# A wait for the landing of the preceding list write, in a fused attention and mixture-of-experts kernel

## The reference

```python
x = layernorm(x + attention(x))        # x: 16 sequences x 256 tokens x 256 features; 16 heads of 16
x = layernorm(x + ffn(x))              # 4096 tokens, 8 experts, 2 experts to a token

# ffn
capacity = ceil(4096 * 2 / 8 * 1.25)   # 1280 slots per expert
gates = softmax(x_flat @ gating_w)
topk_w, topk_idx = top_k(gates, 2)
norm_w = topk_w / (sum(topk_w) + 1e-8)
position = running count of the items of each expert     # the slot of an item
buf[expert, position] = x_flat[token]                    # dropped where position >= capacity
h = relu(buf @ w1 + b1)                                  # 256 -> 1024
out_e = h @ w2 + b2                                      # 1024 -> 256
out[token] += out_e[expert, position] * norm_w           # for both experts of a token
```

## Time and profile before

| | |
|---|---|
| time, median of 3 runs | 821.24 us (820.07 to 822.61) |
| span of the profiled execution | 856.8 us |
| PE, DVE, ACT, POOL busy | 92%, 71%, 52%, 48% of the span |
| mean granted clock of PE | 0.971 of full speed |

### The profile page before, as it was taken

How to read it: one execution, slowest core, us unless ns; L and a number is a source line. 1 busy time by engine, 2 the same in 40 slices (tenths; PEclk the granted TensorE clock), 3 DMA queues, 4 the chain that set the end, 5 groups by cost and what they waited for, 6 DMA issues and landing times.

```text
span 856.8 us, 16628 instructions
## 1 busy us (share of the span) xinstructions
PE 784.5 (92%) x5919; PEld 648.5 (76%) x5919; DVE 605.1 (71%) x1325; ACT 442.1 (52%) x753; POOL 410.2 (48%) x595
## 2 busy tenths in 40 slices
PE   7699989999989985896999999999999999999994
PEld 7577766677667653585889898898898888988993
DVE  5768878888888885683756856756657568665983
ACT  3166757777666664542534534534345345443670
POOL 1011245555555546457146445254364462556675
PEclk9799999999999998799899999999999999999998
DMA  5677765555555572326145245253352451533741
GB/s 158 135 165 161 161 153 113 114 113 114 116 114 110 115 141 73 116 51 180 20 91 109 41 89 115 43 130 50 81 111 40 96 112 31 140 57 57 288 179 46
DMA packets 71534, 92.75 MB, mean 108 GB/s; under 512 B 12972, under 2 KB 55885, under 8 KB 71324
## 3 DMA queue, kind: packets, MB, share of 16 engines
q1 hardware_dynamic: 53308, 67.95, 31.0%
q0 software_dynamic: 16928, 22.15, 14.9%
q10 hardware_dynamic: 1216, 1.57, 0.8%
HBM read 39.18 MB, written 26.89 MB: 77 GB/s over the span
## 4 chain that ended last, share of the span: by engine, by line
PE 69%; DVE 14%; issue 5%; POOL 3%; another core or an unknown queue 3%; DMA 2%; ACT 2%; ACTq 1%; POOLq 0%; DVEq 0%; SPq 0%
PE bank L1718 14%; DVE negm L890 10%; PE wide L1687 8%; PE wide L1685 8%; PE wide L1686 8%; PE bank L985 7%; PE bank L1720 7%; PE wide L1030 5%; PE bank L1664 2%; PE wide L1048 2%; PE bank L1095 2%; PE bank L1064 1%; PE bank L994 1%; POOL slot_list L533 1%
## 5 line engine op out<-in xcount | busy, mean ns | idle before, releaser
L1359 POOL DMA_INDIRECT acc_rows<-o_w,lists x70 | 120.4, 1720 | 181.6 <-ACT o_w L1508 167.9
L890 DVE TENSOR_REDUCE negm<-wide 128x4 f32<-128x1024 f32 x128 | 156.1, 1222 | 50.5 <-PE wide L1030 31.7
L630 ACT ACTIVATE probs<-wide 128x1024 f32<-128x1024 f32 x128 | 131.0, 1024 | 89.1 <-PE wide L1048 68.9
L1475 ACT ACTIVATE h<-wide,b1T 128x512 f32<-128x512 f32 (+1 forms) x200 | 115.0, 600 | 96.8 <-PE wide L1687 69.1
L1720 PE MATMUL bank<-stack,h_lo 128*128 128x256 f32 x560 | 156.9, 280 | 0.0
L1685 PE MATMUL wide<-g_hi,stack 128*128 128x512 f32 (+1 forms) x400 | 140.8, 352 | 5.2 <-DVE g_lo L1536 4.1
L1687 PE MATMUL wide<-g_hi,stack 128*128 128x512 f32 (+1 forms) x400 | 140.1, 350 | 0.1
L1686 PE MATMUL wide<-g_lo,stack 128*128 128x512 f32 (+1 forms) x400 | 140.1, 350 | 0.0
L1508 ACT ACTIVATE o_w<-o_b,lists 128x256 f32<-128x256 f32 x70 | 35.7, 510 | 148.6 <-DVE o_b L1646 135.5
L1718 PE MATMUL bank<-stack,h_hi 128*128 128x512 f32 x304 | 108.7, 401 | 1.3 <-DVE o_b L1646 1.3
L1720 PEld LDWEIGHTS bank<-stack,h_lo 128*128 128x128 f32 x560 | 105.6, 189 | 0.0
(11 more groups left out here) (211 smaller groups left out, 1640.9 us busy)
## 6 DMA issues: line engine op xcount, KB each, us to landing
stack<-qk SPq DMA_DIRECT2D x180, 128.0 KB, 4.2
w_raw<-in_L_ffn_w SPq DMA_DIRECT2D x16, 1024.0 KB
x_sb<-in_L_attn_x SPq DMA_DIRECT2D x16, 256.0 KB, 5.1
x_rows<-x SPq DMA_DIRECT2D x16, 256.0 KB
acc_rows<-x SPq DMA_DIRECT2D x16, 256.0 KB
acc_sb<-acc_rows SPq DMA_DIRECT2D x8, 512.0 KB, 11.1
out<-acc_sb SPq DMA_DIRECT2D x8, 512.0 KB
x_rows<-zrow SPq DMA_DIRECT2D x2, 1152.0 KB, 6.6
```

Of the source, the lines that this page charges most:

```text
L630: nc.scalar.activation(probs[:, i % 4].rearrange("p x c t -> p x (c t)"), shifted_banks(i)[:, :, :], ACT.Exp, scale=SCALE).then_inc(exp_do ...
L890: nc.vector.tensor_reduce(negm[n % 2][:, :, :, u].rearrange("p c x -> p x c"), score_banks(PAIRS * n + u)[:, :, :].rearrange("p x (c t) -> ...
L1359: nc.gpsimd.indirect_dma_start(out=acc_d, out_offset=bass.IndirectOffsetOnAxis(ap=lists[:, e, QC * c + r, 0:1], axis=0), in_=o_w[c][:, r, ...
L1475: ins = nc.scalar.activation(h[u % 2][:, t], banks[BZ[u % 4]][:, t], ACT.Relu, bias=b1T[:, FT * e + f:FT * e + f + 1])
```

## The change

Before each list write of a sequence but its first (c = 0, k = 0), POOL waits until the semaphore of the sequence has the count that it has when all of its earlier writes have landed: 16 for each of the four writes of each earlier sequence on that semaphore, and 16 for each earlier write of this one. Nothing else is changed.

```diff
@@ -530,6 +530,8 @@
                 pool.wait_ge(token_done, m + 1)
                 pool.wait_ge(weight_done, m + 1)
                 for k in range(TOPK):
+                    if c or k:
+                        pool.wait_ge(listed[m % 4], 16 * (QC * TOPK * (m // 4) + TOPK * c + k))
                     nc.gpsimd.indirect_dma_start(
                         out=list_d, out_offset=bass.IndirectOffsetOnAxis(ap=dest[m % 4][:, c, k:k + 1], axis=0),
                         in_=item[m % 4][:, c, k, :], in_offset=None, bounds_check=NE * CAP - 1,
```

## The result

The changed kernel takes 882.79 us (881.62 to 884.7, four runs), the kernel before 821.92 us beside it (820.07 to 822.8): a ratio of 1.0756 [1.0738, 1.0774], 61 us slower. The forecast was slower at 870 us, with a range of 836 to 900.

What follows compares the result with a forecast made beforehand. PE was 92% busy; POOL had about 6.8 us to spare per attention sequence, none in the hand-over. 24 + 28 = 52 us on 856.8 gave 909 us; scaled by 0.9585, 871, stated as 870 us, range 836 to 900.

Steps and rivals of the forecast that it cites:

- both stages pay: Attention and hand-over to the experts: the main forecast, waits cost 24 + 28 us; chance 62%, own range 843 to 888 us.
- pitch: POOL's list writes: start of one write to the next, 4.1 us with the wait in place of 1.27 us.
- The prediction's estimate by the Trainium skill's figure: List writes: fixed 2.0 us with 0.55 us to restart, pitch 2.55 us; sum some 7 us in place of 52.
- Attention stage: One sequence every 20 us: waits exceed POOL's 6.8 us idle, 2.7 us for each of nine sequences, 24 us.
- break-even pitch: Attention stage: pitch up to which POOL's idle time covers three waits a sequence, put at 3.5 us.
- the first rival: Only the hand-over pays: at pitch 3.2 us attention costs 0, the hand-over 12.8 us; 833 us, chance 22%.
- the slack in front of sequence 13's writes: Hand-over: sequence 13's factors had 10 us of slack before their exponential, so ACT stalls only some 3.8 us.
- The last twelve writes: Hand-over, sequences 13 to 15: nine waits make the writes take 39.5 us, where they took 18.56 us.
- The 3 us for the clock: Hand-over: PE waits about 13 us for rows; its clock then drops to the 1.2 GHz level, adding 3 us.
- the hand-over: Stage before the experts, 303 to 400 us: no slack, late list writes delay reload, gathers and PE's rows, 28 us.
- POOL paces everything: Rival for both stages: every pitch stretches to 4.8 us, attention 35 us, hand-over 37 us; 893 us and beyond, chance 12%.
- the waits are nearly met: Rival at the list writes: landings are seen hardly after issue ends, so not slower, 821 us; chance 4%.

Runs made afterwards that it cites:

- further profile: The kernel before, unchanged, profiled once more: 820.48 us, ratio 1.0004, span 818.6 us.
- odd execution: First profiled execution of the unchanged kernel before, the source of the prediction's rows: span 856.8 us.
- earlier trace: Trace of the unchanged kernel before that the prediction read, with its span of 856.8 us; the odd execution.
- The moved writes: Sequence 12's four writes moved behind the factors of 13: in the changed kernel 888.14 us, in the kernel before 824.05 us.

## Why the prediction was right, and where its numbers were off

**What bounds each stage.** As predicted, both stages pay, and the waits act by what is queued behind them on POOL: the cast and the factors in attention, the gathers at the end.

**One wait.** The pitch was taken as 4.1 us, with 1.0 us more for the third landing: 13.3 us for three. Measured on the first ten sequences, the mean pitches are 3.6, 3.8 and 4.7 us, 12.0 us for three. The third is dearer by about the 1.0 us that was added; the base was a little high. The bounds were too narrow: single pitches go from 2.9 to 6.5 us. The further profile of the kernel before gives the same sum directly: a median landing of 3.2 us and the 0.76 us to the next issue are 4.0 us, the mean of the three pitches. The 4.1 us came from the wait behind a 128 KB accumulate, 2.98 us, which is near the 2.9 us measured for 1 KB; no run here tells why the two should agree, so that much was luck.

The Trainium skill ("DMA: Bandwidth & Descriptors", section "Anatomy of one DMA — SWDGE (gpsimd) path") gives such a transfer a fixed cost of about 2.0 us. The changed kernel's landings come near it where the DMA engines are quiet (2.11 us at 403.23, 2.57 us at 238.56) and not where they are busy (4.06 and 5.75 us). The prediction's estimate by the Trainium skill's figure, 7 us in all, fell short.

**Attention stage: right in size by two errors that cancel.** The period of 20.0 us and the idle 6.8 us came from the odd execution; in a usual one they are 18.63 and 5.41 us. With these, 8.27 us from the cast to the first write and 0.97 us of the last one, the break-even pitch is (18.63 - 8.27 - 0.97) / 3 = 3.1 us, not 3.5: the first rival's 3.2 us would have been near it, but the third pitch is 4.7. The loss for one sequence was to be 2.7 us; from the cast at 125.27 us to that at 295.25 us (eight periods of 21.25 us) it is 2.6. The first sequence, put at 0.3 us, lost 5.8 us: its landings were slow (pitches 4.4 to 4.7 us) and its idle time was 3.84 us and not 8.0. So 27.3 us at that cast, in place of 24; the tenth sequence's waits, which the 24 us include, stand behind it and bring 0.7 us more (the first write of sequence 10 moved from 293.11 to 321.16, 28.0 us).

**The step that failed: the slack in front of sequence 13's writes.** "They had 10 us of slack" was read from the earlier trace rows, where the exponential came 10 us behind its factors. There it started 12.0 us after the first of them, in a usual execution 3.4 us (320.85 to 324.22); 1.8 us of these are the two instructions that make the factor it needs, so the slack was 1.5 us at most. ACT's stall is therefore 16.9 us and not 3.8, and the first write of sequence 13 comes 17.1 us later against the first write of 10 (45.20 less 28.05) and not 3.8. The run with the waits of 10 to 12 alone shows this part: 19.6 us.

The moved writes add that the stall is only where the delay is seen; the delay is POOL's. In POOL's own terms the sum comes out. The nine waits of sequences 10 to 12 lengthen these writes by 24.8 us: the nine pitches add up to 36.7 us in place of 11.9, and the forecast's 4.1 us gives 36.9. Against that stood, in the odd execution, 19.4 us of POOL's idle time (6.85, 3.83 and 8.73 us in the earlier trace rows); the further profile has 7.4 (the 6.42 and 1.03 us in the rows above). 24.8 less 7.4 is 17.4 us, and 17.1 were measured. So the waits were rightly sized, and what failed is the idle time set against them.

**The last twelve writes.** 39.5 us were forecast, in place of 18.56; they take 35.2 us (377.17 to 412.38), in place of 18.34. The nine pitches average 3.6 us, below 4.1, since seven of them are 2.9 to 3.3 us (the other two 5.3 and 5.5). That adds 16.9 us in place of 20.9.

**What was to show it.** The idle time before a waiting write is 2.9 us (near 3 was said), that before the cast 0, the period 21.2 us (22.7 was said), ACT waits for POOL's shift, and no write follows another of its sequence after 1.3 us.

**PE's wait and its clock.** The wait for rows is 7.7 us and not 13: the rows come 61.7 us late, and PE's own work by then is 55.1 us late (61.7 and 1.13 less 7.68). The 3 us for the clock are not there: the delay is 61.7 us at the rows and 62.1 us at the end. PE did stand still from 360 to 370 us, with the clock granted at 0.50, the 1.2 GHz level, but then POOL paced the stage.

**The scale.** Multiplying by 0.9585 treated a long span as the rule. In the runs here a span is 1.8 us shorter than its time (818.6 of 820.35, 880.7 of 882.46). Beside the first table it was said that a span is longer than the time; that holds for the odd execution alone. The scaling took 2 us off the sum, and rounding 1.

Together: attention 4.0 us too low with the tenth sequence (28.0 in place of 24), the hand-over 5.7 (33.7 in place of 28), scale and rounding 3: about the 13 us by which 870 us missed 882.8. The hand-over's 5.7 is again a sum of errors that partly cancel: 13.3 us too low ahead of sequence 13's writes, 4.0 too high in the last twelve, 3 too high for the clock; the rest is rounding and 0.4 us at PE's rows. Of the rivals, the one in which POOL paces everything was right in its name, as in either stage POOL has hardly any idle time left but landings. Its condition is not met: the mean pitch is 4.0 us in attention and 3.6 in the last twelve writes, not 4.8. That the waits are nearly met falls: the shortest idle time before a write that directly follows another of its sequence is 1.9 us.

## What to carry to other kernels

In this kernel a wait for one's own transfer cost next to nothing while it fitted into the idle time of the queue that holds it, and in full beyond that; so find that idle time for one period, and count the landings against it, with the landing as it is at that place. Two transfers in flight in place of one, with 32 waits in place of 48, gave nearly all of the time back here (3.9 us lost in place of 61). Take a base period from a profile whose span agrees with the runs. Where it doesn't, the odd execution's idle times and slacks are the first numbers to distrust, and waits for a releaser outside of the program a sign to look for.

## What was not expected of the hardware

The same 1 KB indirect write took 2.11 to 5.75 us from issue to landing within one execution, and POOL needed about 0.76 us from the landing to the next issue. A wait whose count was already there showed no cost at all (the idle time stayed at 0.30 us). And one profiled execution of an unchanged kernel was 38 us longer than another, with a period of 20.0 in place of 18.63 us in its attention stage from 123 us on and waits that the profile calls "remote"; its cause stays open.
